# A decoder layer on one core: layer norms applied on GpSimd, and a reordered opening

## What is computed

```python
def _layernorm(x, axis=-1, eps=1e-05):
    return (x - m) / jnp.sqrt(v + eps)
x = x + attn(_layernorm(x), wq, wk, wv, wo)          # causal, 2 heads, RoPE
x = x + xattn(_layernorm(x), ctx, ctx, Wq, Wk, Wv, Wo, bq, bk, bv, bo)   # 16 heads, 1601 keys
x = x + ffn(_layernorm(x), W1, b1, W2, b2, scale)    # GELU, low-rank additions from tokens 1 to 16
```

## Time and profile before

| | us |
|---|---|
| median of three runs | 447.05 (446.14 to 458.3) |
| the profiled execution | 447.47 |
| its span, first to last instruction | 445.7 |

### The profile page before, as it was taken

How to read it: one execution, slowest core, us unless ns; L and a number is a source line. 1 busy time by engine, 2 the same in 40 slices (tenths; PEclk the granted TensorE clock), 3 DMA queues, 4 the chain that set the end, 5 groups by cost and what they waited for, 6 DMA issues and landing times.

```text
span 445.7 us, 9617 instructions
## 1 busy us (share of the span) xinstructions
PE 378.0 (85%) x3640; PEld 175.5 (39%) x3640; DVE 322.0 (72%) x706; ACT 298.6 (67%) x624; POOL 120.4 (27%) x189
## 2 busy tenths in 40 slices
PE   0723798998999998997999998989998999989956
PEld 0421443343344443432444544433544443443325
DVE  2533478969689988877789778898897789874022
ACT  1411013886588878854779878767889888979932
POOL 4541100258300012554700012675300003300010
PEclk9965655999699999967899999998999999999988
DMA  7062236003511712043306033044120231000000
GB/s 259 7 221 80 91 126 219 2 1 112 174 39 54 182 37 88 1 159 112 97 7 157 27 95 91 2 159 163 50 85 25 77 110 50 1 13 3 1 1 12
DMA packets 22316, 35.57 MB, mean 80 GB/s; under 512 B 1622, under 2 KB 19814, under 8 KB 22270
## 3 DMA queue, kind: packets, MB, share of 16 engines
q1 hardware_dynamic: 22270, 34.95, 24.5%
HBM read 19.15 MB, written 11.96 MB: 70 GB/s over the span
## 4 chain that ended last, share of the span: by engine, by line
PE 58%; DVE 21%; ACT 10%; issue 5%; POOL 2%; DMA 2%; SPq 1%; POOLq 0%; ACTq 0%; DVEq 0%
PE wsum L952 19%; DVE part_max L648 12%; PE score L966 12%; PE ring L983 8%; ACT probs L823 5%; PE ring L1077 4%; PE ring L1070 2%; DVE xn L742 2%; PE ring L1119 2%; PE ring L1019 2%; DVE xn L765 2%; PE ring L1110 2%; PE ring L1008 1%; ACT q_unit L834 1%; PE ring L1002 1%
## 5 line engine op out<-in xcount | busy, mean ns | idle before, releaser
L648 DVE TENSOR_REDUCE part_max<-ring 128x1 f32<-128x401 f32 x512 | 260.5, 567 | 52.9 <-PE ring L983 52.3
L823 ACT ACTIVATE probs<-score 128x512 f32<-128x512 f32 (+1 forms) x416 | 223.0, 597 | 56.0 <-PE score L966 53.2
L983 PE MATMUL ring<-k_unit,q_unit 51*128 51x401 bf16 x512 | 148.6, 362 | 10.9 <-DVE part_max L648 7.3
L952 PE MATMUL wsum<-probs,v_unit 128*32 128x256 f32 (+1 forms) x1664 | 139.5, 406 | 2.7 <-ACT unit_ctx L828 2.1
L966 PE MATMUL score<-q_unit,k_unit 51*128 51x256 bf16 (+1 forms) x832 | 127.9, 284 | 9.0 <-ACT probs L823 6.6
L966 PEld LDWEIGHTS score<-q_unit,k_unit 51*128 51x128 bf16 (+1 forms) x832 | 47.5, 98 | 106.2 <-ACT probs L823 60.4
L983 PEld LDWEIGHTS ring<-k_unit,q_unit 51*128 51x128 bf16 x512 | 48.6, 97 | 32.9 <-DVE part_max L648 21.3
L952 PEld LDWEIGHTS wsum<-probs,v_unit 128*32 128x32 f32 (+1 forms) x1664 | 34.8, 110 | 52.9 <-issue 27.4
L526 POOL TENSOR_TENSOR max_parts<-neg_max,c_sb 128x8 bf16<-128x8 f32 x16 | 3.3, 209 | 150.3 <-DVE neg_max L652 150.3
L878 ACT ACTIVATE v_aug<-ring 128x128 f32<-128x128 f32 x48 | 9.4, 283 | 25.3 <-PE ring L1077 25.3
L1008 PE MATMUL ring<-c_sb,xn 128*128 128x128 f32 x24 | 6.2, 350 | 20.8 <-DVE xn L674 12.8
(11 more groups left out here) (106 smaller groups left out, 323.4 us busy)
## 6 DMA issues: line engine op xcount, KB each, us to landing
k_unit<-k_rows SPq DMA_DIRECT2D x32, 300.2 KB
v_unit<-v_aug SPq DMA_DIRECT2D x16, 234.0 KB, 5.8
ctx_sb<-ctx_t SPq DMA_DIRECT2D x4, 800.5 KB, 7.3
k_rows<-k_parts SPq DMA_DIRECT2D x4, 601.5 KB, 3.5
k_rows<-k_parts SPq DMA_DIRECT2D x4, 599.2 KB, 3.7
k_rows<-k_parts SPq DMA_DIRECT2D x4, 401.0 KB, 4.1
k_rows<-k_parts SPq DMA_DIRECT2D x4, 399.5 KB, 4.3
q_unit<-q_rows SPq DMA_DIRECT2D x32, 48.0 KB
```

The costliest lines, as they stand in the source:

```text
L648: v_.tensor_reduce(part_max[:, par, q, head, hp, c:c + 1], ring[s][:, 0:CW], AX.X, ALU.max)\
L823: a_.activation(probs[0:rows, i % PB, :], score[i % EB][0:rows, :], ACT.Exp)\
L952: last = mm(wsum[32 * j:32 * j + 32, 0:S], v_unit[0:rows, u, VQ * t + VW * j:VQ * t + VW * j + 32], probs[0:rows, i % PB, S * (j // 2):S * ...
L983: mm(ring[s][:, 0:CW], q_unit[rows, u, hp, P * q:P * (q + 1)], k_unit[rows, u, L * hp + (CW - 1) * c:L * hp + (CW - 1) * c + CW], start=Tr ...
```

## The change

Norm 1 of batches 1 to 3, norm 2 of batches 1 to 3 and norm 3 of batches 0 to 2 are applied on GpSimd. Norms 2 and 3 stand there right behind their power, so their items leave `SIDE`; norm 1 stands at its item. In the opening the first two tiles of x are measured, and their power made, ahead of the other six. One list, `FIRST`, replaces the two: norm 1 of batch 1 comes second, the softmax of batch 0 and its scaling, now on VectorE, come ahead of keys 2 and 3, and two steps of batch 1 come ahead of the turn of the softmax. The queries of unit 0 no longer go through memory: a new item "pick" multiplies their parts with a table of zeros and ones (128 x 384 words more in the second constants load) into one bank, and ScalarE copies it into `q_unit`; unit 0 of batch 0 then waits for its two key loads alone. The value projections of batch 0 become seven items of two tiles (`U0` to `U6`), after each four maxima.

```diff
@@ -71,10 +71,10 @@
                         ("cos", 2 * S), ("sin", 2 * S), ("mask", 3 * P),
-                        ("select", 16), ("blocks", 4), ("ones", L), ("zeros", S)])
+                        ("select", 16), ("blocks", 4), ("pick", 3 * P), ("ones", L), ("zeros", S)])
 W_FIRST = W_COLS["Wv"][1]
 C_FIRST = C_COLS["zero"][1]
-C_HELD = C_COLS["blocks"][1]
+C_HELD = C_COLS["pick"][1]
@@ -105,6 +105,13 @@
     put("blocks", np.eye(4, dtype=np.float32))
+    pick = np.zeros((P, 2, 3, P), np.uint16)
+    for hp in range(2):
+        for par in range(2):
+            for t, part in enumerate(Q_PART):
+                for d in range(DX):
+                    pick[2 * DX * par + 2 * d + hp, hp, part, HALF * par + MR + DX * t + d] = 0x3F80
+    put("pick", pick.view(np.float32))
     put("ones", np.full((MR, L), TWO_ONES, np.float32))
@@ -126,9 +133,9 @@
     (0, 9): [("prep", "K0", 1)], (0, 10): [("prep", "pT0", 1), ("prep", "pT1", 1)], (0, 11): [("prep", "K1", 1)],
-    (0, 12): [("prep", "av", 1), ("post", "ln3", -1)],
+    (0, 12): [("prep", "av", 1)],
     (1, 0): [("prep", "K2", 1)], (1, 1): [("prep", "wo", 1), ("post", "x3T", -1)], (1, 3): [("prep", "K3", 1)],
-    (1, 4): [("prep", "ln2", 1), ("prep", "store0", 1)], (1, 6): [("prep", "x2T", 1)],
+    (1, 4): [("prep", "store0", 1)], (1, 6): [("prep", "x2T", 1)],
     (1, 8): [("prep", "q", 1), ("prep", "store1", 1)], (1, 9): [("prep", "split", 1)],
@@ -136,13 +143,14 @@
 SIDE_LAST = {
-    (0, 6): [("post", "OT", -1)], (0, 8): [("post", "Wo", -1)], (0, 11): [("post", "ln3", -1)],
+    (0, 6): [("post", "OT", -1)], (0, 8): [("post", "Wo", -1)],
     (1, 0): [("post", "x3T", -1)], (1, 3): [("post", "low", -1)], (1, 10): [("post", "h0", -1), ("post", "h1", -1)],
...
 }
-PREP_FIRST = ["ln1", "xT", "qk", "qks", "K0", "K1", "e0", "e1", "K2", "K3", "store0", "soft", "pn", "v", "pT0", "pT1",
-              "av", "store1", "wo", "ln2", "x2T", "q", "split"]
-PREP_SECOND = ["ln1", "xT", "qk", "qks"]
+FIRST = [("ln1", 0), ("ln1", 1), ("xT", 0), ("qk", 0), ("qks", 0), ("K0", 0), ("K1", 0), ("e0", 0), ("e1", 0), ("soft", 0),
+         ("pn", 0), ("K2", 0), ("K3", 0), ("store0", 0), ("v", 0), ("xT", 1), ("qk", 1), ("pT0", 0), ("pT1", 0), ("av", 0),
+         ("store1", 0), ("wo", 0), ("ln2", 0), ("x2T", 0), ("q", 0), ("split", 0), ("qks", 1), ("pick", 0)]
 POST_LAST = ["OT", "Wo", "ln3", "x3T", "low0", "low1", "h0", "h1", "out"]
@@ -198,11 +206,11 @@
-    plan = [("prep", name, 0) for name in PREP_FIRST] + [("prep", name, 1) for name in PREP_SECOND]
-    for i in range(4):
-        plan += [("M", 0, k) for k in range(8 * i, 8 * i + 8)] + [("prep", f"V{i}", 0)]
-    plan += [("prep", "load", 0), ("ctx", 1)] + [("M", 1, k) for k in range(4)] + [("mT", 0)]
-    return plan + [("M", 1, k) for k in range(4, AHEAD_FIRST)]
+    plan = [("prep", *what) for what in FIRST]
+    for i in range(7):
+        plan += [("M", 0, k) for k in range(4 * i, 4 * i + 4)] + [("prep", f"U{i}", 0)]
+    plan += [("M", 0, k) for k in range(28, MU)] + [("prep", "load", 0), ("ctx", 1)]
+    return plan + [("M", 1, k) for k in range(4)] + [("mT", 0)] + [("M", 1, k) for k in range(4, AHEAD_FIRST)]
@@ -223,6 +231,18 @@
 RING = ring_slots()
+def last_values(b):
+    return ("prep", "V3" if b else "U6", b)
+def value_tiles(name):
+    width = 4 if name[0] == "V" else 2
+    t0 = width * int(name[1])
+    return t0, min(width, KT_FULL - t0), t0 + width > KT_FULL
@@ -430,7 +450,7 @@
                 if u == 0:
-                    s, n = RING["prep", "V3", b]
+                    s, n = RING[last_values(b)]
                     sp.wait_ge(drained[s], n + 1)
@@ -474,8 +494,9 @@
                                 .then_inc(queries_written, 16)
-                        load_queries(b, 0)
-                        if b == 0:
+                        if b:
+                            load_queries(b, 0)
+                        else:
                             load_rest(b)
@@ -512,12 +533,13 @@
             pool.wait_ge(consts_in, 16)
-            pool.wait_ge(mv1_set, B * QT)
-            g.tensor_scalar(var1[:, :], mv1[:, :, :, 1].rearrange("p b q -> p (b q)"), EPS, None, ALU.add)\
-                .then_inc(var1_set, 1)
-            pool.wait_ge(var1_set, 1)
-            g.tensor_tensor(rstd1[:, :, :].rearrange("p b q -> p (b q)"), var1[:, :], C("pow"), ALU.pow)\
-                .then_inc(rstd1_set, 1)
+            for i, (t0, t1) in enumerate(((0, QT), (QT, B * QT))):
+                pool.wait_ge(mv1_set, t1)
+                g.tensor_scalar(var1[:, t0:t1], mv1[:, :, :, 1].rearrange("p b q -> p (b q)")[:, t0:t1], EPS, None, ALU.add)\
+                    .then_inc(var1_set, 1)
+                pool.wait_ge(var1_set, i + 1)
+                g.tensor_tensor(rstd1[:, :, :].rearrange("p b q -> p (b q)")[:, t0:t1], var1[:, t0:t1],
+                                C("pow")[:, t0:t1], ALU.pow).then_inc(rstd1_set, 1)
             pool.wait_ge(weights_in, 16)
@@ -544,7 +566,15 @@
                     name, b = item[1:]
-                    if name == "K1" or name == "K3" and b:
+                    if name == "ln1" and b:
+                        s, n = RING["prep", "xT", b - 1]
+                        pool.wait_ge(filled[s], n + 1)
+                        pool.wait_ge(rstd1_set, 2)
+                        for q in range(QT):
+                            last = g.tensor_scalar(xn1[:, q, :], x_all[:, b, q, :], mv1[:, b, q, 0:1],
+                                                   rstd1[:, b, q:q + 1], ALU.subtract, ALU.mult)
+                        last.then_inc(xn1_done, 1)
+                    elif name == "K1" or name == "K3" and b:
@@ -565,6 +595,12 @@
                         g.tensor_tensor(rstd2[:, :], var2[:, :], C("pow")[:, 0:QT], ALU.pow).then_inc(rstd2_set, 1)
+                        if b:
+                            pool.wait_ge(rstd2_set, b + 1)
+                            for q in range(QT):
+                                last = g.tensor_scalar(xn2[:, q, :], x1[:, q, :], mv2[:, q, 0:1], rstd2[:, q:q + 1],
+                                                       ALU.subtract, ALU.mult)
+                            last.then_inc(xn2_done, 1)
                         g.tensor_tensor(x1_bo[:, b, :, :], x1[:, :, :],
@@ -578,7 +614,7 @@
                             .then_inc(q_split, 1)
-                    elif name == "pn":
+                    elif name == "pn" and b:
                         pool.wait_ge(prsum_done, b + 1)
@@ -598,6 +634,12 @@
                     g.tensor_tensor(rstd3[:, :], var3[:, :], C("pow")[:, 0:QT], ALU.pow).then_inc(rstd3_set, 1)
+                    if b < B - 1:
+                        pool.wait_ge(rstd3_set, b + 1)
+                        for q in range(QT):
+                            last = g.tensor_scalar(xn3[:, q, :], x2[:, q, :], mv3[:, q, 0:1], rstd3[:, q:q + 1],
+                                                   ALU.subtract, ALU.mult)
+                        last.then_inc(xn3_done, 1)
                     g.tensor_tensor(x2_b2[:, :, :], x2[:, :, :],
@@ -624,11 +666,12 @@
             dve.wait_ge(x_in, 16)
-            for i in range(B * QT):
-                v_.bn_stats(stats1[:, i, :], x_all[:, i // QT, i % QT, :]).then_inc(stats1_set, 1)
-            for i in range(B * QT):
-                dve.wait_ge(stats1_set, i + 1)
-                v_.bn_aggr(mv1[:, i // QT, i % QT, :], stats1[:, i, :]).then_inc(mv1_set, 1)
+            for tiles in (range(QT), range(QT, B * QT)):
+                for i in tiles:
+                    v_.bn_stats(stats1[:, i, :], x_all[:, i // QT, i % QT, :]).then_inc(stats1_set, 1)
+                for i in tiles:
+                    dve.wait_ge(stats1_set, i + 1)
+                    v_.bn_aggr(mv1[:, i // QT, i % QT, :], stats1[:, i, :]).then_inc(mv1_set, 1)
             dve.wait_ge(consts_in, 16)
@@ -668,7 +711,7 @@
                 name, nb = item[1:]
-                if name == "ln1":
+                if name == "ln1" and nb == 0:
                     dve.wait_ge(rstd1_set, 1)
@@ -722,6 +765,14 @@
                     v_.reciprocal(prob_rsum[:, :, :], prob_sum[:, :, :]).then_inc(prsum_done, 1)
+                    if nb == 0:
+                        dve.wait_ge(prsum_done, 1)
+                        for q in range(QT):
+                            cols = slice(0, P) if q == 0 else slice(P, 3 * P)
+                            for h in range(HA):
+                                last = v_.tensor_scalar(prob_norm[:, h, cols], prob_self[:, h, cols],
+                                                        prob_rsum[:, q, h:h + 1], None, ALU.mult)
+                        last.then_inc(norm_done, 1)
                 elif name == "wo":
@@ -864,25 +915,28 @@
                         .then_inc(drained[s], 1)
-                elif name in ("V0", "V1", "V2", "V3"):
-                    if name == "V0":
+                elif name[0] in "UV":
+                    if name[1] == "0":
                         act.wait_ge(pads_set, 1)
...
```

(30 more changed lines are left out.)

4 lines of the change are left out of this document (2 added, 2 removed).

## The result

The changed kernel takes 420.15 us (median of 4 executions, 420.03 to 423.25). Against the kernel before on the same chip that is a ratio of 0.938 (95% interval 0.927 to 0.949): 6% faster. Its profiled execution took 420.15 us with a span of 418.3, beside 447.47 and 445.7 before. Forecast were 416.3 us, in a range of 410 to 428.

What follows compares the result with a forecast made beforehand. TensorE bounds ordinary stages, VectorE normalizes behind GpSimd plus lower clock three long ones, a serial chain the opening. Span 445.7 less 9.4, 2.6, 18.7 and 0.4, plus 0.3, is 414.9 us; forecast 416.3, range 410 to 428.

Steps and rivals of the forecast that it cites:

- The sum: Whole kernel: span 445.7 less 9.4, 2.6, 18.7 and 0.4, plus 0.3, gives 414.9 us; forecast time 416.3.
- Norms to GpSimd: Three long stages where the next batch's keys are made: moving norms 2 and 3 off VectorE saves 18.7 us.
- Norm 1 of batches 2 and 3: A tight stage: taking this norm off VectorE saves 0.4 us, bounds 0 to 0.6.
- The price on GpSimd: Norms 2 and 3 take GpSimd 0.9 us each time; second hidden, third just fits before the maxima's splits; 0.3 us booked.
- rival 4: Change is slower: GpSimd's third norm delays the maxima's parts, TensorE waits, clock falls and would have to spread; 2%.
- Two tiles first: Opening: VectorE reaches the first normalize earlier; 0.8 us saved, 1.8 if a power doesn't block.
- Softmax on VectorE: Opening: scaling ahead of VectorE's key split lets the transposes start at 25.0 instead of 29.12, 4.1 us saved.
- The keys: Opening: keys land as before, last traffic at 40 to 41 us; first maximum matmul taken at 40.8.
- Values in pairs: Unit 0's maxima: value matmuls in pairs leave VectorE idle 0.15 us, seven times; 2.6 us saved.
- Rival 1: Clock still dips once or twice, costing 5 us or 2 to 4: 419 to 426 us; 15%.
- The signs of being wrong: Clock keeps dips where keys are split, first maxima wait for the keys' landing, or score stages wait for GpSimd.

## Why the prediction was right, step by step
- **The sum.** Mechanism and size were right for the two large terms, but that the time lies so near the forecast is in part luck. Of the span 30.8 us were to be saved; the profiles show 27.4 and 30.5. The norms brought 2.9 us more than booked and the opening 0.8 more; in the other direction stand 2.2 us at three turns of the maxima, a late dip of 3.8 us in one of the two profiles, and about 1 us in small pieces, where the sum had a saving of 0.1.
- **Norms to GpSimd.** Right in mechanism, shown three ways: with this part alone, undone, and by re-making the collision with instructions of no other effect. Its 18.7 us were 21.6, since the stages came out at 22.3, 22.2 and 22.2 us and not 23.2: the idle time of an ordinary stage, 1.9 us, was put in, and they have 0.4 to 0.9. In the ordinary stage TensorE waits 1.3 us for ScalarE's exponentials and 0.5 for VectorE; in the long ones only 0.4 and 0.2, and that in one of them.
- **Norm 1 of batches 2 and 3.** 0.4 us were taken; the tight stage is 18.18 us before and after. Nothing was saved.
- **The price on GpSimd.** The term that was furthest off for its size: 0.3 us booked in all, measured 0.34 twice and 1.5 in the last batch. A pair was taken at 0.9 us and measures 1.6, since the row taken had two multiplies and the normalize has a subtraction. Behind the second norm it was hidden as forecast. At the third, the 0.34 us are the price alone, as they are gone with the pair at 0.9. The 1.5 are mostly the place: the slack of 0.9 was read in the stage at 162 and taken for all three, but in the last batch TensorE waited 0.8 us at this turn already before the change. What rival 4 describes did happen here: the parts came late and TensorE waited at its turn, 2.5 us. In the changed kernel's two profiles the clock stayed up behind this wait, in six others it fell; so the cost was 1.5 us there and up to 8 in a variant. It did not spread, and the change stayed far from slower.
- **Two tiles first.** 0.8 us was taken, since the second normalize would meet the power over six columns. Both were over at 7.63, and the power began at 7.57, behind the sum over six columns with its 0.38 us. The upper bound, 1.8, was passed: TensorE's first turn comes at 7.78 instead of 10.04.
- **Softmax on VectorE.** As forecast its first scaling waits for GpSimd's split, which ends at 19.46 + 1.70 = 21.16, and the four take 2.17 us. They end at 21.96, and TensorE's moved projections, 21.10 + 1.13 = 22.23, at nearly the same time; the transposes begin at 22.07 instead of 25.0. That is early by 2.0 us, since ScalarE was done with its copies sooner and the projections began at 21.10 and not at 23.1, and by 0.8 since they took 1.13 us at the higher clock, not 1.9.
- **The keys.** The forecast named their landing as what could hold the first maximum, and it did, 1.5 us behind the pick. At 38.6 they still landed 2 us earlier than taken, as their loads were issued at 30.33 instead of 32.74.
- **Values in pairs.** 2.6 us forecast, 1.3 measured: a pair takes 1.22 us at the lower clock, more than half of 2.07, and VectorE idles 0.31 to 0.37 us behind each of six pairs, not 0.15 behind seven.
- **The clock.** Rival 1, a dip or two that stays, had 15%. One did appear, in the last batch, where the kernel before had none in its profile; in the second profile of the changed kernel that stage took 18.7 us instead of 22.5 and the span was 415.2, beside the 414.9 of the sum. Which stages of the last batch hold a dip changes from execution to execution of one kernel, and it goes with the spread: by their mean clocks, the executions of the changed kernel at 417 to 420 us had it low for 48 to 59 us, those at 423 to 425 for 65 to 68. The sum gave no term to it.
- **The signs of being wrong.** Three were named. The clock keeps no dips where keys are split. But the first maxima did wait for the keys' landing, 1.5 us, and TensorE did wait for GpSimd, 2.5 us in the last batch. Both were small beside the gain; as signs they had needed a size.

## What to carry to other kernels
Where VectorE and GpSimd work at the same time, look at the duration of each form of VectorE instruction next to GpSimd's. Here one form, two operations from SBUF to SBUF, took up to 1.87 us instead of 0.34 beside a long GpSimd instruction, while the maxima out of PSUM kept to 0.54 to 0.58. Moving that form was enough: to the other engine (long stages of 22.3, 22.2 and 22.2 us), or, with less gain, ahead of the long GpSimd work (23.5, 23.5 and 24.9). Price a short wait of TensorE by the clock line too: of the 4 to 11 us that each long stage lost, 1.6 to 8.6 lay in the clock behind the wait and not in the wait, and one wait of 2.5 us in the last batch was followed by low clock in six profiles of eight. An operation priced from a row needs the row's operators as well as its size, and slack read at one place must be read at every place where the sum uses it.

## What was not expected of the hardware
GpSimd's two-operation instruction over 128x128 words takes 0.45 us with two multiplies or with an addition and a multiply, and 0.80 us where one of the two operations is a subtraction, first or second. And the same TensorE wait of 2.5 us was followed by 0, 3.4, 13.7 or 17.1 us at the lower clock in different profiles. What decides between them is open; so is what makes the low stretch of the opening last 41 us in some executions and 55 in others with the same opening.
